# Full exponentials in two SBUF buffers in place of the score banks, in a Perceiver block

## The reference, cut to what matters

```python
x = layer_norm(image_embeds, ln1_g, ln1_b)          # (16, 1601, 128)
l = layer_norm(latents, ln2_g, ln2_b)               # (16, 64, 128)
q = l @ Wq
kv = jnp.concatenate([x, l], axis=1) @ Wkv
k, v = jnp.split(kv, 2, axis=-1)                    # 16 heads of 64
w = softmax(einsum('bhqd,bhkd->bhqk', q * scale, k * scale))
out = einsum('bhqk,bhkd->bhqd', w, v)               # then @ Wo
```

## Time and profile before

| | |
|---|---|
| median of three runs | 954.18 us (952.11 to 957.75) |
| the profiled execution | 957.0 us, of it 955.3 us span |
| mean granted TensorE clock | 0.983 of full speed |
| TensorE (PE) busy | 914.2 us, 96% |
| VectorE (DVE) busy | 800.5 us, 84% |
| ScalarE (ACT) busy | 701.9 us, 73% |
| GpSimd (POOL) busy | 378.7 us, 40% |

### The profile page before, as it was taken

How to read it: one execution, slowest core, us unless ns; L and a number is a source line. 1 busy time by engine, 2 the same in 40 slices (tenths; PEclk the granted TensorE clock), 3 DMA queues, 4 the chain that set the end, 5 groups by cost and what they waited for, 6 DMA issues and landing times.

```text
span 955.3 us, 20495 instructions
## 1 busy us (share of the span) xinstructions
PE 914.2 (96%) x8246; PEld 491.1 (51%) x8246; DVE 800.5 (84%) x1591; ACT 701.9 (73%) x1003; POOL 378.7 (40%) x378
## 2 busy tenths in 40 slices
PE   8679999999999999999999999999999999999977
PEld 5444444545454545454545454545454545567653
DVE  5979797979798989898989898989897876498986
ACT  4756878787878787878787878787878677664633
POOL 6472034343434343434343434343434231354443
PEclk9889999999999999999999999999999999999987
DMA  6403030303030303030303030303020200000000
GB/s 213 83 1 71 1 93 2 93 2 75 22 74 21 74 22 73 22 73 22 73 23 72 23 72 24 73 23 72 23 60 23 38 23 24 1 24 24 2 2 22
DMA packets 74565, 41.95 MB, mean 44 GB/s; under 512 B 62276, under 2 KB 69864, under 8 KB 74472
## 3 DMA queue, kind: packets, MB, share of 16 engines
q1 hardware_dynamic: 74184, 39.60, 16.9%
q10 hardware_dynamic: 288, 1.05, 0.3%
HBM read 25.98 MB, written 0.59 MB: 28 GB/s over the span
## 4 chain that ended last, share of the span: by engine, by line
PE 81%; DVE 13%; ACT 3%; issue 2%; DMA 1%; POOL 0%; DVEq 0%; ACTq 0%
PE S L2141 10%; PE S L2132 9%; PE OA L2165 9%; PE OA L2168 9%; PE OA L2171 9%; PE S L2135 9%; PE WW L2075 8%; PE S L1217 2%; PE WW L2102 1%; PE WW L2103 1%; PE WW L2104 1%; DVE amx L802 1%; PE WW L2062 1%; PE WW L2063 1%; PE WW L2064 1%
## 5 line engine op out<-in xcount | busy, mean ns | idle before, releaser
L1849 ACT ACTIVATE region<-S,sigma 128x1024 f16<-128x1024 f32 x208 | 231.8, 1114 | 137.7 <-PE S L2141 137.7
L1530 DVE TENSOR_TENSOR region<-S,region 128x1024 f16<-128x1024 f32 x208 | 252.3, 1213 | 44.2 <-ACT S L1853 44.1
L1518 DVE TENSOR_REDUCE mx<-WW 128x1 f32<-128x512 f32 (+1 forms) x480 | 262.4, 583 | 29.7 <-PE WW L2075 22.4
L1853 ACT ACTIVATE S<-S,sigma 128x1024 f32<-128x1024 f32 x208 | 224.5, 1079 | 0.0
L1662 POOL TENSOR_TENSOR xk<-raw,xk 128x508 f16<-128x508 f32 x64 | 63.3, 999 | 168.1 <-DVE xk L1397 168.1
L2075 PE MATMUL WW<-xT,region 128*128 128x512 f16 x360 | 124.8, 381 | 4.4 <-DVE region L1509 2.1
L2132 PE MATMUL S<-region,xT 128*128 128x512 f16 (+1 forms) x416 | 124.5, 380 | 2.4 <-DVE region L1530 1.7
L2165 PE MATMUL OA<-region,xk 128*128 128x512 f16 (+1 forms) x416 | 123.8, 379 | 0.0
L2135 PE MATMUL S<-region,xT 128*128 128x512 f16 (+1 forms) x416 | 123.7, 379 | 0.0
L2141 PE MATMUL S<-region,xT 128*128 128x512 f16 (+1 forms) x416 | 123.7, 379 | 0.0
L2168 PE MATMUL OA<-region,xk 128*128 128x512 f16 (+1 forms) x416 | 123.7, 379 | 0.0
(11 more groups left out here) (314 smaller groups left out, 1836.6 us busy)
## 6 DMA issues: line engine op xcount, KB each, us to landing
raw<-ctx SPq DMA_DIRECT2D x16, 768.0 KB
rb<-inv_dram SPq DMA_DIRECT2D x16, 512.0 KB, 3.7
xT<-xk SPq DMA_TRANSPOSE x48, 3.1
left_row<-left_pT SPq DMA_DIRECT2D x48, 2.0 KB
raw<-ctx SPq DMA_DIRECT2D x16, 32.5 KB
WO_lo<-L_xattn_Wq ACTq DMA_DIRECT2D x1, 512.0 KB, 3.8
WO_hi<-L_xattn_Wkv ACTq DMA_DIRECT2D x1, 512.0 KB, 4.7
lx<-x SPq DMA_DIRECT2D x1, 512.0 KB, 7.1
```

The lines of the kernel that those rows point to most:

```text
L1518: nc.vector.tensor_reduce(mx[:, r, c:c + 1], W[BANK[("m", n)]][:, 0:width], AX.X, ALU.max)\
L1530: nc.vector.tensor_tensor(p_lo[k], src, p_hi[k], ALU.subtract).then_inc(lo_done.sem, 1)
L1849: nc.scalar.activation(p_hi[k], src, ACT.Exp, scale=sigma[:, 0:1])
L1853: nc.scalar.activation(src, src, ACT.Exp, scale=sigma[:, 0:1]).then_inc(e_done.sem, 1)
```

## The change

The full exponential is written to one of two new SBUF buffers of 128x1024 f32 (`e_full`) in place of the score banks that it was read from. The low part reads it there, so both of its inputs are in SBUF. The scores of u wait for the full exponential of u-2 (`e_done`), not for its low part (`lo_done`). The full exponential of u has a new wait, for the low part of u-2, which frees its buffer. `weigh` waits as before. Nothing else is changed: the order of instructions on each engine, their number and their sizes stay.

```diff
@@ -193,6 +193,8 @@
         o_sb = part(8192, 2048).rearrange("p (k n) -> p k n", k=2)
+
+        e_full = [sb(f"e_full{k}", [128, COLS]) for k in range(2)]
 
@@ -368,6 +370,9 @@
+        def e_buffer(turn, u):
+            return e_full[(turn.off * UNITS + u) % 2][:]
 
@@ -1526,8 +1531,7 @@
                 k = pbuf(turn, u)
                 dve.wait_ge(e_done.sem, e_done.upto(turn, u))
-                src = score_banks(turn, u).rearrange("p a n -> p (a n)")
-                nc.vector.tensor_tensor(p_lo[k], src, p_hi[k], ALU.subtract).then_inc(lo_done.sem, 1)
+                nc.vector.tensor_tensor(p_lo[k], e_buffer(turn, u), p_hi[k], ALU.subtract).then_inc(lo_done.sem, 1)
 
@@ -1849,8 +1853,11 @@
             def exponentials_full(turn, u):
+
                 src = score_banks(turn, u).rearrange("p a n -> p (a n)")
-                nc.scalar.activation(src, src, ACT.Exp, scale=sigma[:, 0:1]).then_inc(e_done.sem, 1)
+                if not (turn.off == 0 and u < 2):
+                    act.wait_ge(lo_done.sem, lo_done.upto(turn, u - 2))
+                nc.scalar.activation(e_buffer(turn, u), src, ACT.Exp, scale=sigma[:, 0:1]).then_inc(e_done.sem, 1)
 
@@ -2108,7 +2115,7 @@
             def scores(turn, u):
                 p = turn.off % 2
                 if not (turn.off == 0 and u < 2):
-                    pe.wait_ge(lo_done.sem, lo_done.upto(turn, u - 2))
+                    pe.wait_ge(e_done.sem, e_done.upto(turn, u - 2))
```

## The result

The changed kernel takes 1000.41 us (median of 4 runs, 999.69 to 1002.5) against 955.96 us for the kernel before in the same comparison: a ratio of 1.0466, 95% interval 1.0436 to 1.0496. It is 44 us slower. The forecast was 987 us, with an own range of 970 to 1005 and a whole range of 958 to 1014.

The account below looks back on a forecast made before the run. TensorE was taken as the bound, busy 47.97 of 48 us a slot. From 957.0 us: -1.7 (score wait), +13.4 and +20.6 (VectorE-GpSimd collisions), -2.8 (profiled run above median) gave 987 us; own range 970 to 1005, whole 958 to 1014.

Parts of the forecast that it names:

- Place A: Unit 1, slots 0 to 13: low(1) starts 0.05 us behind a GpSimd subtraction, ends 0.96 us late; 13.4 us in all.
- R2: Rival: VectorE wins at Place A, GpSimd waits and that place costs nothing; 973 us, chance 0.15.
- Place B: Units 7 to 9, slots 1 to 15: GpSimd's normalisation and output subtraction make low(9) 1.47 us late; 14 slots, 20.6 us.
- Place C: low(10) against the second GpSimd output subtraction, a tie; taken as VectorE first, no loss; otherwise 1.8 us more per slot.
- R1: Rival: GpSimd wins the tie at Place C, 25 us more in all; 1012 us, chance 0.21.
- Part 2: ScalarE writes its full exponential to SBUF, with a new wait for low(u-2); at most 7 us of ScalarE, covered: 0.
- the length of the low part: VectorE's low part with two SBUF inputs stays at 1.21 us, within 0.07 us: 0.
- R3: Rival: no blocking between VectorE's low part and GpSimd, only Part 1 is left; 952.5 us, no change, chance 0.12.
- R4: Rival: low part 0.07 us shorter from SBUF, blocking rare, TensorE gains 2 to 4 us; 949 us, chance 0.07.
- The pow: GpSimd's pow (L1651) doesn't block VectorE, counted at 0; if it did, 0.4 us a slot at low(5), 6 us.
- Part 1: Scores wait for the full exponential, not the low part; removes TensorE's idle time in 2 places, both last slot: -1.7 us.
- The sum: 957.0 - 1.7 + 13.4 + 20.6 = 989.3 us, less 2.8 for the profiled execution: 986.5, say 987 us.

Follow-up runs that it names:

- x4: Changed kernel with the last statistic of unit 0 moved behind the low part of unit 1 on VectorE: 989.58 us, ratio 1.0333 to the kernel before.
- x1: Changed kernel with the scores of u waiting for the low part of u-2 again: 999.34 us, ratio 1.0429 to the kernel before.
- x5: Changed kernel with GpSimd's output subtractions waiting for the low part of unit 9: 977.89 us, ratio 1.0245 to the kernel before.
- x2: Changed kernel with the low part reading the score banks and the scores waiting for it again, exponential still to SBUF: 957.37 us, ratio 0.9988.
- x3: Changed kernel with memsets in place of GpSimd's split subtractions, multiplications and output subtractions in the slots: 952.93 us, ratio 0.9947 to the kernel before.
- x7: Changed kernel with the statistic between low(2) and the bank of q(1) moved behind q(1): 993.69 us, ratio 1.0403 to the kernel before.
- x6: Changed kernel with two statistics moved around low(1) and low(2), GpSimd's output subtractions in four behind low(9) to low(11): 965.38 us, ratio 1.0096.

## Why the prediction was right, and where it was off

**Place A** (forecast 0.96 us in each of 14 slots): measured 1.00 in slots 2 to 13. The tight pair of VectorE and TensorE passed it on undiminished. R2 (VectorE wins) is refuted there: low(1) took 2.18 or 2.19 us in each of them. In slot 14 VectorE does start first, by 0.16 us, and TensorE loses 0.37 us, as in x4. **Place B** (forecast 1.47): measured 1.5 to 1.6, of it 0.06 to 0.26 ahead of unit 10, from low(8), and 1.4 from low(9), in slots 1 to 14. The forecast slot was 50.3 us, the measured one is 50.38. x1 to x5 show the mechanism from each side: take away the second SBUF input, or GpSimd's reads, or the overlap in time, and the matching part of the loss is gone.

**Place C** (the tie): VectorE won it in 13 of 14 slots, as taken, but by 0.03 to 0.05 us in twelve of them and 0.11 in slot 3. The rows of before put GpSimd 0.02 us from the other outcome, so that this came out as forecast was luck. In slot 14, which has no statistics, GpSimd came 0.72 us ahead:

```profile
814.54 2.13 POOL L555 TENSOR_TENSOR ew<-region,o_hi 128x1024 f16<-128x1024 f32 x1 [1.88 <-ACT o_hi L1834]
815.26 2.49 DVE L1534 TENSOR_TENSOR region<-e_full,region 128x1024 f16<-128x1024 f32 x1
```

That cost TensorE 0.9 us. R1 was thus the rival closest to coming true: by the prediction's price of 1.8 us a slot, leads of 0.05 us decided over 20 us. No run shows that price, since in no slot did GpSimd win by so little.

**Part 2** and the length of the low part (both 0): right. x2 shows the first, and the second by the median of 1216 ns. R3 and R4 are refuted, and with them the estimate of 65 ns less from SBUF that was worked out from the cycle counts of the Trainium skill ("VectorE: DVE Perf Modes", the TRN2 errata): the median with two SBUF inputs is 1216 ns, the mean with one from PSUM 1213.

**The pow** (counted at 0): right for what it costs, but the pow itself is held. In slot 6 it takes 3.35 us behind low(4) where it took 2.43 in the kernel before:

```profile
391.45 1.22 DVE L1534 TENSOR_TENSOR region<-e_full,region 128x1024 f16<-128x1024 f32 x1
391.62 3.35 POOL L1655 TENSOR_TENSOR smc<-smc,mhalf 128x13 f32<-128x13 f32 x1 [4.06 <-DVE smc L464]
394.72 1.21 DVE L1534 TENSOR_TENSOR region<-e_full,region 128x1024 f16<-128x1024 f32 x1
```

It is so in 13 slots, and GpSimd's idle time covers the 0.9 us. By the trace the pow ends at 394.97, and low(5), which starts 0.25 us before that, isn't held. So not every GpSimd instruction with SBUF inputs holds VectorE to its very end; why this one doesn't is open.

The rule of the Trainium skill that a VectorE instruction with two SBUF inputs contends with a GpSimd one that reads SBUF, not with one that only writes it ("SBUF — State Buffer", Who interferes with whom) agrees with x3 in both halves: 1.21 us beside a memset, 3.25 us beside the one large addition that was kept (below).

**Part 1** (forecast -1.7 us) is the step that failed in kind. I put the two score waits of the earlier trace rows in the last slot, from small margins there. They were elsewhere: in the trace of before they are

```profile
70.33 0.39 PE L2132 MATMUL S<-region,xT 128*128 128x512 f16 x1 [1.04 <-DVE region L1530]
119.53 0.39 PE L2132 MATMUL S<-region,xT 128*128 128x512 f16 x1 [0.68 <-DVE region L1530]
```

that is, in unit 2 of slots 0 and 1, where VectorE is behind as a whole. The change removed both, and the very next wait for VectorE, for the bank of q(1), took them over: it was 1.05 us in slot 0 before and is now

```profile
79.36 0.39 PE L2082 MATMUL WW<-xT,region 128*128 128x512 f16 x1 [2.27 <-DVE region L1514]
```

A wait that went because TensorE was let past a late engine came back at the next thing that this engine had to deliver. In slot 0 the new total is 1.0 us more, place A alone. The last slot gained 0.17 us by unit 10, not 1.7. There part 1 is worth something that the prediction didn't name: low(0) is held to 3.24 us (last section) at no cost to TensorE, where in x1, with the old wait, TensorE waits 1.59 us for it.

**The sum** came out 10 us low: forecast +32.3, measured +42.7 on the span (998.0 against 955.3). By the starts of the slots in both traces:

| | forecast | measured |
|---|---|---|
| ahead of slot 0 | 0 | +1.1 |
| slot 0 | +1.0 | +1.0 |
| slot 1 | +2.4 | +4.1 |
| slots 2 to 13 | +29.2 | +30.5 |
| slot 14 | +1.5 | +2.8 |
| last slot, to its last scores | -1.7 | +2.1 |
| behind that | 0 | +1.1 |

Some 1.3 us of the excess is spread over slots 2 to 13; the rest lies at both ends.

In slot 1 part 1 turned against itself. Place A and the wait that part 1 had moved fall together at the bank of q(1), and TensorE waits 2.30 us there, where it waited 1.05 before. Right behind this wait its granted clock is 0.50 of full speed, the lower of its two levels (1.2 in place of 2.4 GHz), for 3.3 us (columns of the second line as in the earlier trace rows):

```profile
129.56 0.61 PE L2082 MATMUL WW<-xT,region 128*128 128x512 f16 x1 [2.30 <-DVE region L1514]
129.56:132.90 3.34, 3.33 (x8) 1.19 (x9) 1.44 (x3) 0.00 (x0) 2.86 (x3) 0.50 0.74 139
```

Half of 3.34 us is 1.7, the excess of the slot. It isn't chance from run to run: over the same 8 us of slot 1 the mean granted clock is 0.79 in the changed kernel, in x5 and in x7 (waits of 2.30, 2.30 and 2.10 us). It is 1.00 in the kernel before, in x4 (a wait of 1.69 us), in x6, and in x1, where the idle time comes in four pieces of at most 1.06 us; in these slot 1 has no such excess. It is no plain matter of one wait's length: behind the 2.27 us in slot 0 and the 2.28 us in slot 3 the clock stayed at 1.00, while in x1 the stretch with the 2.19 us of slot 3 and the one behind it have 0.79 and 0.78, and this is the slot that is 1.3 us longer there. The prediction had no term for the clock.

In slot 14 it is 0.9 us of place C and 0.4 of place A, which the sum had in slots 0 to 13 only. In the last slot I counted low parts as harmless, having no maxima behind them, and so missed the early self-attention work that VectorE has in this slot (Kx, L801). It comes behind low(9), which is held there too (2.51 us), and TensorE waits 1.98 us for it. In x5, where low(9) is free, it still waits 0.91 us, so low(9) is only part of that. The 1.1 us ahead of slot 0 weren't followed up: slot 0 starts at 64.3 to 66.5 us over all traces, the kernel before at 65.2. Nor was the 1.1 us behind the last scores.

## What to carry to other kernels

Moving one input of this VectorE tensor_tensor from PSUM to SBUF didn't change its length by itself, but gave it two SBUF inputs and so coupled it to GpSimd, beside which it had run untouched. Before such a move, lay the timelines of the two engines side by side: an overlap can cost the later one the rest of the earlier (the pow above is the one exception seen). Whether that reaches the end time is read from the margins between VectorE and TensorE, here 0.06 us at the shared banks; and a wait that is relaxed on a saturated engine pays only if the engine waited for has nothing else to deliver soon. In slot 1 several short waits were also cheaper than about the same idle time in two longer ones, by the clock that was granted after them.

## What was not expected of the hardware

A GpSimd instruction on a single partition holds up a VectorE instruction on all 128. L527 adds two rows of 1x1024; in the last slot the low part began 0.19 us behind it, and ended 1.08 us after it:

```profile
829.04 2.35 POOL L527 TENSOR_TENSOR srow<-region 1x1024 f32<-1x1024 f32 x1 [12.36 <-ACT region L1871]
829.23 3.24 DVE L1534 TENSOR_TENSOR region<-e_full,region 128x1024 f16<-128x1024 f32 x1
```

In the kernel before the same pair stood 0.18 us apart and the low part took 1.21 us. The hold stays in x3 (3.25 us), where this addition was kept. And the order of arrival is decided by leads as small as 0.03 us (412.91 against 412.94), with an outcome that repeated in 13 slots.
